# A routed mixture of experts on one core: the second layer with the rows on the partitions

## What is computed

```python
logits = (xf @ Wr + br) / TAU
top_val, top_idx = jax.lax.top_k(logits, 2)
top_w = jax.nn.softmax(top_val, axis=-1)
w = jnp.einsum('nke,nk->ne', jax.nn.one_hot(top_idx, E), top_w)
h = jnp.einsum('nd,edh->enh', xf, We1) + be1[:, None, :]      # 128 -> 768
a, g = jnp.split(h, 2, axis=-1)
act = a * gelu(g)
yE = jnp.einsum('enh,ehd->end', act, We2) + be2[:, None, :]   # 384 -> 128
yr = jnp.einsum('end,ne->nd', yE, w)
x = x + layernorm(ys + yr)
```

## Time and profile before

| | us |
|---|---|
| runs shown | 1186.52, 1187.3, 1191.24 |
| median | 1187.3 |
| the profiled execution: its own time | 1182.42 |
| its span, first to last instruction | 1180.7 |
| busy in the span: PE, DVE, ACT, POOL | 1019.0, 830.3, 742.6, 632.6 |

### The profile page before, as it was taken

How to read it: one execution, slowest core, us unless ns; L and a number is a source line. 1 busy time by engine, 2 the same in 40 slices (tenths; PEclk the granted TensorE clock), 3 DMA queues, 4 the chain that set the end, 5 groups by cost and what they waited for, 6 DMA issues and landing times. The chain is left out here.

```text
span 1180.7 us, 31510 instructions
## 1 busy us (share of the span) xinstructions
PE 1019.0 (86%) x8446; PEld 608.8 (52%) x8446; DVE 830.3 (70%) x2411; ACT 742.6 (63%) x1311; POOL 632.6 (54%) x1195
## 2 busy tenths in 40 slices
PE   4488888988888898987788998866999999999875
PEld 3453333333333333333345665535888888888732
DVE  5677887778777877777779998433666666666637
ACT  4577777777777767775655666414666666666616
POOL 4236666666666666664423777771444444444344
PEclk9899999999999999998996999878999999999988
DMA  8313333333332333333243111112222222221166
GB/s 217 94 47 93 99 96 103 95 100 87 97 108 86 99 95 99 100 99 111 71 150 115 54 54 57 54 60 68 61 64 64 64 58 63 62 65 54 43 224 210
DMA packets 135606, 107.47 MB, mean 91 GB/s; under 512 B 32203, under 2 KB 127874, under 8 KB 135538
## 3 DMA queue, kind: packets, MB, share of 16 engines
q1 hardware_dynamic: 124722, 87.45, 26.3%
q0 software_dynamic: 8544, 17.78, 4.2%
q10 hardware_dynamic: 2272, 1.45, 0.4%
HBM read 55.96 MB, written 50.69 MB: 90 GB/s over the span
## 5 line engine op out<-in xcount | busy, mean ns | idle before, releaser
L1542 DVE TENSOR_REDUCE maxima<-ps 128x8 f32<-128x1024 f32 x320 | 381.2, 1220 | 119.4 <-PE ps L1164 107.3
L916 ACT ACTIVATE pT_area<-ps 128x1024 f32<-128x1024 f32 x320 | 327.1, 1024 | 138.0 <-PE ps L1196 136.8
L704 POOL TENSOR_SCALAR_AFFINE_SELECT pT_area<-pT_area 128x256 f32<-128x256 f32 (+1 forms) x448 | 190.3, 439 | 103.7 <-ACT pT_area L916 103.2
L806 POOL DMA_INDIRECT ys_dram<-quad_area,place_cur x139 | 133.0, 957 | 192.6 <-issue 135.7
L1237 PE MATMUL ps<-pT_area,quad_area 128*32 128x512 f32 (+3 forms) x2048 | 190.7, 446 | 0.0
L796 POOL DMA_INDIRECT xs_dram<-quad_area,idx_cur x128 | 123.1, 962 | 74.9 <-issue 73.6
L1196 PE MATMUL ps<-quad_area 64*128 64x512 bf16 (+3 forms) x1024 | 125.5, 302 | 39.4 <-DVE maxima L1542 37.9
L1404 PE MATMUL ps<-quad_area 128*128 128x256 f32 (+1 forms) x456 | 130.0, 367 | 6.3 <-issue 4.5
L1405 PE MATMUL ps<-quad_area 128*128 128x256 f32 (+1 forms) x456 | 128.5, 364 | 0.0
L1164 PE MATMUL ps<-quad_area 61*128 61x128 bf16 (+2 forms) x1792 | 126.2, 242 | 0.0
L1024 ACT ACTIVATE xnT<-ps,be_cur 128x256 f32<-128x256 f32 (+1 forms) x228 | 94.4, 447 | 47.6 <-PE ps L1405 47.3
(11 more groups left out here) (237 smaller groups left out, 1523.1 us busy)
## 6 DMA issues: line engine op xcount, KB each, us to landing
qk_dram<-split_area SPq DMA_DIRECT2D x192, 128.0 KB, 2.3
quad_area<-qk_dram SPq DMA_DIRECT2D x256, 96.0 KB, 2.3
row_area<-xs_dram SPq DMA_DIRECT2D x63, 132.0 KB
pT_area<-ys_dram SPq DMA_DIRECT2D x16, 512.0 KB, 5.0
pT_area<-in_L_ffn_We SPq DMA_DIRECT2D x12, 384.0 KB, 7.0
out_dram<-pT_area SPq DMA_DIRECT2D x7, 512.0 KB, 2.9
xs_dram<-row_area SPq DMA_DIRECT2D x5, 528.0 KB, 4.2
split_area<-in_L_ffn_We SPq DMA_DIRECT2D x12, 192.0 KB, 3.6
```

Source lines behind the costliest of these rows:

```text
L704: return pool.affine_select(out=blocks, in_=blocks, compare_op=ALU.is_ge, fill=0.0, base=0, pattern=[[0, count], [1, P]], channel_multipli ...
L806: pool.indirect_dma_start(ys_dram, at, ys[:, ns % 2, h, :], None).then_inc(s_yst[ns % 2], 16)
L916: act.activation(pT[:, gs % 2, n, :], ps[:, bank:bank + 2, :].rearrange("p a b -> p (a b)"), ACT.Exp).then_inc(s_exp, 1)
L1542: dve.tensor_reduce(to, ps[:, bank:bank + 2, :].rearrange("p a (j k) -> p a j k", k=P), AX, ALU.max).then_inc(s_mxf, 1)
```

## The change

The experts' second layer swaps its operands: the hidden numbers are stationary, 128 rows at a time, and the weights `w2_cur` move, so a pair takes six matmuls of 128 columns instead of three of 256, and the result has the rows on the partitions at once. It goes into two PSUM banks in turn (`Y_BANKS`). The turn back (L1424), ACT's copy to `ysT` (L1034) and the wait chain through them go. The bias, which stood on the partitions, now stands along the columns: `be2` is loaded once, repeated on all partitions (`be2_all`, 128x1536, one DMA more on SP behind the weights), DVE copies the tile's 128 columns to `be2_cur` in each step, and the weighting becomes two operations, an add of the bias and a multiplication by the weight in place. `be_cur` loses a column. `routed_as` has four operations instead of five.

The order of a step changes on three engines. PE turns the rows of tile s+1 ahead of the first layer of tile s. ACT reads the next expert's number and copies the turned rows ahead of its gelus. DVE starts with the copies of the second-layer weights and bias of tile s, goes on with the three hidden products, weights tile s-2, and ends with `routed_as` of tile s+1, which waits for the scatter of tile s-3.

The diff, without the counts and names that follow from it (semaphores, buffers, waits on the number of small loads):

```diff
@@ -57,7 +57,7 @@
-YT_BANK, Y_BANK = 6, 7
+Y_BANKS = (6, 7)
@@ -217,7 +217,8 @@
-yT = v_flat[:, 1024:2048].rearrange("p (a t) -> p a t", a=2)
+yT = v_flat[:, 512:1536].rearrange("p (a t) -> p a t", a=2)
+be2_all = v_flat[:, 1536:1536 + E * C]
@@ -568,6 +569,8 @@
+    sp.dma_start(be2_all, a["L0_ffn_be2"].rearrange("(o e) c -> o (e c)", o=1).broadcast_to([P, E * C])).then_inc(s_we, 16)
+
@@ -799,7 +802,7 @@
-            pool.wait_ge(s_wt, 5 * n - 8)
+            pool.wait_ge(s_wt, 4 * n - 7)
@@ -1000,15 +1003,16 @@
-    act.activation(beT[:, :, 7], iota_f[:, ROUTED:ROUTED + E], ACT.Copy)
-    act.activation(beT[:, :, 6], ps[:, BE_TURN, 6 * E:7 * E], ACT.Copy).then_inc(s_beTsb, 1)
+    act.activation(beT[:, :, 6], iota_f[:, ROUTED:ROUTED + E], ACT.Copy).then_inc(s_beTsb, 1)
...
-    act.wait_ge(s_we, 16 * 2 * E)
-
-    def copy_w1(ns, n):
-        e = act.value_load(etile[0:1, bass.ds(n, 1)], min_val=0, max_val=E - 1)
+    act.wait_ge(s_we, 16 * (2 * E + 1))
+
+    def expert_of(n):
+        return act.value_load(etile[0:1, bass.ds(n, 1)], min_val=0, max_val=E - 1)
+
+    def copy_w1(ns, e):
@@ -1016,6 +1020,9 @@
     def expert_tile(ns, n):
+        if ns + 1 < ROUTED:
+            e = expert_of(n + 1)
+            copy_xsT(ns + 1, n + 1)
         if ns < ROUTED:
@@ -1024,17 +1031,9 @@
                 act.activation(gelE[:, ring, 0:width(ns)], ps[:, ring, 0:width(ns)], ACT.Gelu,
                                bias=be_cur[:, ns % 8, 3 + k:4 + k]).then_inc(s_ge, 1)
                 if k == 0 and ns + 1 < ROUTED:
-                    copy_w1(ns + 1, n + 1)
-        if ns + 1 < ROUTED:
-            copy_xsT(ns + 1, n + 1)
-        if 0 <= ns - 1 < ROUTED:
-
-            act.wait_ge(s_yeT, n)
-            w = width(ns - 1)
-            act.activation(ysT[:, (ns - 1) % 2, 0:w], ps[:, YT_BANK, 0:w], ACT.Identity,
-                           bias=be_cur[:, (ns - 1) % 8, 6:7]).then_inc(s_yeTsb, 1)
-
-    copy_w1(0, 0)
+                    copy_w1(ns + 1, e)
+
+    copy_w1(0, expert_of(0))
     copy_xsT(0, 0)
     expert_steps(act, expert_tile)
@@ -1393,6 +1392,8 @@
     def expert_tile(ns, n):
+        if ns + 1 < ROUTED:
+            turn_rows(ns + 1, n + 1)
         if ns < ROUTED:
@@ -1404,24 +1405,17 @@
                           start=True, stop=True).then_inc(s_he, 1)
-        if ns + 1 < ROUTED:
-            turn_rows(ns + 1, n + 1)
         if 0 <= ns - 1 < ROUTED:
-            par, w = (ns - 1) % 2, width(ns - 1)
+            par = (ns - 1) % 2
             pe.wait_ge(s_w2c, n)
-            ge(pe, s_yeTsb, n - 1)
+            ge(pe, s_yeb, n - 2)
             for k in range(CHUNKS):
                 pe.wait_ge(s_hide, CHUNKS * (n - 1) + k + 1)
-                last = pe.matmul(ps[:, YT_BANK, 0:w], w2_cur[:, par, k * P:(k + 1) * P], hidT[:, par, k, 0:w],
-                                 start=(k == 0), stop=(k == CHUNKS - 1))
-            last.then_inc(s_yeT, 1)
-        if 0 <= ns - 2 < ROUTED:
-
-            pe.wait_ge(s_yeTsb, n - 1)
-            ge(pe, s_yesb, n - 2)
-            for h in range(halves(ns - 2)):
-                last = pe.transpose(ps[:, Y_BANK, h * P:(h + 1) * P], ysT[:, ns % 2, h * P:(h + 1) * P], ident[:])
+                for h in range(halves(ns - 1)):
+                    last = pe.matmul(ps[:, Y_BANKS[par], h * C:(h + 1) * C], hidT[:, par, k, h * P:(h + 1) * P],
+                                     w2_cur[:, par, k * C:(k + 1) * C], start=(k == 0 and h == 0),
+                                     stop=(k == CHUNKS - 1 and h == halves(ns - 1) - 1))
             last.then_inc(s_ye, 1)
@@ -1812,47 +1806,58 @@
         ring, h = ns % 4, slice(0, halves(ns))
         to, other = weight_cur[:, ring, h], weight_other[:, ring, h]
-        second = xs[:, ring, h, SECOND_E]
+        second_e, expert = xs[:, ring, h, SECOND_E], be_cur[:, ns % 8, 6:7]
         dve.wait_ge(s_xs[ring], 32 * (n // 4 + 1) if isinstance(n, int) else 8 * (n - ring) + 32)
-        dve.tensor_scalar(second, second, be_cur[:, ns % 8, 7:8], None, ALU.is_equal).then_inc(s_wt, 1)
-        wait_apart(dve, s_wt, 5 * n + 1, s_passed)
         if ns >= 4:
             wait_apart(dve, s_yst[ns % 2], stored(ns - 4, n - 4), s_passed)
-        dve.tensor_tensor(place_cur[:, ring, h], xs[:, ring, h, PLACE], second, ALU.add).then_inc(s_wt, 1)
-        dve.tensor_tensor(to, xs[:, ring, h, SECOND_W], second, ALU.mult).then_inc(s_wt, 1)
-        dve.scalar_tensor_tensor(out=other, in0=second, scalar=0.0, in1=xs[:, ring, h, FIRST_W],
+        dve.scalar_tensor_tensor(out=place_cur[:, ring, h], in0=second_e, scalar=expert, in1=xs[:, ring, h, PLACE],
+                                 op0=ALU.is_equal, op1=ALU.add).then_inc(s_wt, 1)
+        dve.scalar_tensor_tensor(out=to, in0=second_e, scalar=expert, in1=xs[:, ring, h, SECOND_W],
                                  op0=ALU.is_equal, op1=ALU.mult).then_inc(s_wt, 1)
-        wait_apart(dve, s_wt, 5 * n + 4, s_passed)
+        dve.scalar_tensor_tensor(out=other, in0=second_e, scalar=expert, in1=xs[:, ring, h, FIRST_W],
+                                 op0=ALU.not_equal, op1=ALU.mult).then_inc(s_wt, 1)
+        wait_apart(dve, s_wt, 4 * n + 3, s_passed)
         dve.tensor_tensor(to, to, other, ALU.add).then_inc(s_wt, 1)
+
+    def copy_second(ns, n):
+
+        ge(dve, s_ye, n - 1)
+        e = dve.value_load(etile[0:1, bass.ds(n, 1)], min_val=0, max_val=E - 1)
+        dve.tensor_copy(w2_cur[:, ns % 2, :], we2[:, bass.ds(e * HR, HR)]).then_inc(s_w2c, 1)
+        dve.tensor_copy(be2_cur[:, ns % 4, :], be2_all[:, bass.ds(e * C, C)]).then_inc(s_b2c, 1)
     def expert_tile(ns, n):
         if ns < ROUTED:
             par, w = ns % 2, width(ns)
-            routed_as(ns, n)
+            copy_second(ns, n)
             for k in range(CHUNKS):
                 ring = (CHUNKS * ns + k) % H_BANKS
                 dve.wait_ge(s_ge, CHUNKS * n + k + 1)
-                if k == 0:
-                    ge(dve, s_yeT, n - 1)
                 dve.scalar_tensor_tensor(out=hidT[:, par, k, 0:w], in0=ps[:, ring, RT:RT + w], scalar=be_cur[:, ns % 8, k:k + 1],
                                          in1=gelE[:, ring, 0:w], op0=ALU.add, op1=ALU.mult).then_inc(s_hide, 1)
-            ge(dve, s_yeT, n - 1)
-            e = dve.value_load(etile[0:1, bass.ds(n, 1)], min_val=0, max_val=E - 1)
-            dve.tensor_copy(w2_cur[:, par, :], we2[:, bass.ds(e * HR, HR)]).then_inc(s_w2c, 1)
         if 0 <= ns - 2:
-
-            par, h = ns % 2, halves(ns - 2)
-            dve.wait_ge(s_ye, n - 1)
-            wait_apart(dve, s_wt, 5 * n - 5, s_passed)
-            if ns >= 4:
-                dve.wait_ge(s_yst[par], stored(ns - 4, n - 4))
-            dve.tensor_tensor(ys[:, par, 0:h], ps[:, Y_BANK, 0:P * h].rearrange("p (h c) -> p h c", h=h),
-                              weight_cur[:, (ns - 2) % 4, 0:h].rearrange("p (h o) -> p h o", o=1).broadcast_to([P, h, C]),
-                              ALU.mult).then_inc(s_yesb, 1)
-
-    dve.wait_ge(s_we, 16 * 2 * E)
+            weigh(ns - 2, n - 2)
+        if ns + 1 < ROUTED:
+            routed_as(ns + 1, n + 1)
+
+    def weigh(ns, n):
+
+        par, h = ns % 2, halves(ns)
+        to, w = ys[:, par, 0:h], weight_cur[:, ns % 4, 0:h]
+        bias = be2_cur[:, ns % 4].rearrange("p (o c) -> p o c", o=1).broadcast_to([P, h, C])
+        dve.wait_ge(s_ye, n + 1)
+        wait_apart(dve, s_b2c, n + 1, s_passed)
+        wait_apart(dve, s_wt, 4 * n + 4, s_passed)
+        if ns >= 2:
+            dve.wait_ge(s_yst[par], stored(ns - 2, n - 2))
+        dve.tensor_tensor(to, ps[:, Y_BANKS[par], 0:C * h].rearrange("p (h c) -> p h c", h=h), bias, ALU.add).then_inc(s_yeb, 1)
+        wait_apart(dve, s_yeb, n + 1, s_passed)
+        dve.tensor_tensor(to, to, w.rearrange("p (h o) -> p h o", o=1).broadcast_to([P, h, C]), ALU.mult).then_inc(s_yesb, 1)
+
+    dve.wait_ge(s_we, 16 * (2 * E + 1))
     for par in range(2):
         dve.wait_ge(s_scat[par], 8 * R * B)
+    routed_as(0, 0)
     expert_steps(dve, expert_tile)
```

More of the change, by code:

```diff
@@ L256, in build @@
         outT = outT_area[:, 0:2 * T].rearrange("p (a t) -> p a t", a=2)
-        be_rows = sb("be_rows", [E * 7, P])
-        beT = sb("beT", [P, E, 8])
-        be_cur = sb("be_cur", [P, 8, 8])
+        be_rows = sb("be_rows", [E * 6, P])
+        beT = sb("beT", [P, E, 7])
+        be_cur = sb("be_cur", [P, 8, 7])
         rows_cur = quad_area[:, 0:DEPTH * NT * ROW].rearrange("p (a t c) -> p a t c", a=DEPTH, c=ROW)
@@ L265, in build @@
         hidT = quad_area[:, 0:2 * CHUNKS * RT].rearrange("p (a k t) -> p a k t", a=2, k=CHUNKS)
-        xsT, ysT = (quad_area[:, at:at + 2 * RT].rearrange("p (a t) -> p a t", a=2) for at in (2048, 3072))
+        xsT = quad_area[:, 2048:2048 + 2 * RT].rearrange("p (a t) -> p a t", a=2)
         ys = quad_area[:, 4096:4096 + 2 * RT].rearrange("p (a h c) -> p a h c", a=2, h=2)
@@ L269, in build @@
         w2_cur = outT_area[:, 0:2 * HR].rearrange("p (a x) -> p a x", a=2)
```

(20 more changed lines are left out.)

## The result

The changed kernel takes 1204.74 us, median of four runs (1201.76 to 1206.77), against 1186.91 for the kernel before on the same chip: a ratio of 1.0158, 95% interval 1.0135 to 1.018. It is slower by 1.6%; the forecast was 0.9%, and of the 17.8 us between the two medians it had summed up 10.4. The profiled execution took 1205.39 us, of which 1203.6 is span.

A forecast was written before the change was run, and what follows sets the result against it. PE was taken to bound the pairs before, DVE's loops through the scatter after. Pairs +2, handover +1.5, singles +3.9, drain +1.5 and late scatters +1.5 made +10.4: 1192.8 profiled, 1197.7 us median, range 1182 to 1209.

The forecast's parts named there:

- With both loops turning: Pairs: the one-step loop holds the row load where the two-step loop needs it, so steps take about 4.36 us.
- Loop two: Two steps: weighting, scatter, place (4.84 to 5.42 us), then DVE's stretch to the next weighting (3.71): 4.28 to 4.57 a step.
- the pairs: 60 steps of the experts' stage, two tiles' weightings apart: 4.36 us against 4.33, so +2 us (-3 to +10).
- loop one: One step: place, routing, SP's row load, delayed scatter, next place; 4.24 to 4.30 us before, 4.30 to 4.36 after.
- PE's 4.15 can't be had while this loop stands: Pairs: the one-step loop through row load and scatter, 4.30 to 4.36 us, keeps PE from its 4.15 step.
- Rival A: PE sets the pace: scatter clear of the row load, pairs at 4.15 us, singles break even; 1176.5 us, chance 0.12.
- about where they meet: Pairs: 4.36 us a step, where the one-step and two-step loops through the scatter were taken to meet.
- late scatters: Around the loop's exit a few scatters land late, no longer hidden by PE's pace: +1.5 us (0 to 4).
- The singles: Nine steps after the pairs: DVE takes over from ACT's chain, 3.3 us a step against 2.87, so +3.9 us.
- Handover and drain: Last pair to first single, 11.7 us against 10.2; last singles to last landing, 10.4 against 8.9: +1.5 each.
- PE's saving: Pairs: PE's step falls from 4.33 to 4.15 us, 0.18 less, 10.8 over 60 steps if PE sets the pace.
- Rival C: DVE's two copies hold up POOL's scatter issue by 0.56 us, pairs +13 in place of +2; 1209 us, chance 0.15.

The follow-up runs named there:

- e3: Changed kernel, with SP's row load also waiting for the scatter of tile s-4, so it starts after that landing: 1193.32 us, ratio 1.0071 to the kernel before.
- e1: Changed kernel with eight slots for the places instead of four, so a place waits for the scatter of eight tiles earlier: 1180.44 us, ratio 0.9959 to the kernel before.
- e2: Changed kernel with DVE's register load issued behind the hidden products, a step ahead of the copies using it; four slots: 1181.42 us, ratio 0.9964 to the kernel before.
- e5: Changed kernel with DVE's register load and both copies put back behind the hidden products; four slots: 1177.25 us, ratio 0.9935 to the kernel before.
- e4: Changed kernel with both eight slots for the places and the register load behind the hidden products: 1170.03 us, ratio 0.9872 to the kernel before.
- e8: Changed kernel with DVE's register load done twice in a row ahead of the copies: 1221.89 us, ratio 1.0306 to the kernel before.
- e7: Changed kernel with eight slots and early register load, but rows turned behind the first layer and copied behind ACT's gelus: 1170.12 us, ratio 0.9876 to the kernel before.

## Why the prediction was right, and where it was off

The direction was forecast, and so was the wait that binds; the size was not: +10.4 us were summed, and the stage took 18.9 more.

**What binds.** "With both loops turning" was half right. Loop two binds as described, and its stretch measures as summed: place to weighting 3.66 and 3.76 against 3.71. The parts err both ways: place to the end of the register load is 1.51 (908.34 to 909.85) against 0.55 + 0.7, the copies 0.41 (909.85 to 910.26) against 0.56, the hidden products 1.18 against 1.28, add to multiplication 0.56 against 0.62. e3 shows that the scatter and its collision with the row load are the other half of that loop, e1 that without the wait nothing of the pairs' loss is left.

**The step that failed is loop one:** "PE's 4.15 can't be had while this loop stands". It stands unchanged in e2 and e5, and PE has its 4.15 to 4.2 there. Its two rows showed the row load holding up a place by 2.6 to 2.7; that the load, coming later step by step, falls behind the scatter and lets a place through was not thought of. Rival A named an escape by an earlier row load; e3 makes that one by hand, and e2 and e5 show one by a later. The trace of before has the later one too, behind a weighting at 861.77 (SP and DVE):

```profile
864.94 0.38 SPq L582 DMA_DIRECT2D row_area<-xs_dram  x1
...
866.97 0.16 DVE L1821 TENSOR_TENSOR place_cur<-row_area 128x2 int32<-128x2 f32 x1 [0.26 <-DVE row_area L1817]
```

The row load starts 3.17 behind the weighting, and the place comes 2.03 behind the row load without waiting for the scatter, where the prediction held that no row shows less than 2.6. It is rare there: PE's 4.33 is longer than loop one's 4.24 to 4.30, so the row load mostly drifts the other way, from 2.80 behind the weighting (tile 21) to 2.35 (tile 28).

**The term that was mis-sized is the pairs.** 4.36, "about where they meet", came from that loop. Loop two by itself was summed at 4.28 to 4.57, and the steady steps from tile 14 to tile 54 measure 4.435, with 5.17 from a weighting to its place and 3.70 from there to the next weighting: the scatter is caught by the row load in part in most steps, about half of the way from 4.84 to 5.42. That is +6.6 us over 60 steps where +2 was put down, inside the bounds of 4.28 to 4.50. On top of it come the late scatters of the first and last steps, +4.4 where +1.5 was put down, just over the 4 allowed: the 14 steps from tile 0 take 65.5 us where 14 of 4.435 are 62.1, and the six from tile 54 to 60 take 27.6 for 26.6.

**The singles** were forecast at 3.3 and take 3.43 a step, by the chain through DVE's queue that was forecast. In the changed kernel's DVE timeline:

```profile
1117.56 0.29 DVE L1855 TENSOR_TENSOR quad_area<-quad_area,weight_cur 128x128 f32<-128x128 f32 x1
...
1119.15 0.60 DVE L1826 COPY outT_area<-split_area 128x384 f32 x1 [0.60 <-PE ps L1416]
...
1120.99 0.29 DVE L1855 TENSOR_TENSOR quad_area<-quad_area,weight_cur 128x128 f32<-128x128 f32 x1
```

The prediction's terms add up to 3.3 to 3.5, of which it took the lower end. The copy of 0.36 takes 0.60 there, which it didn't have, and the gap of the register load is 0.60 in place of 0.7; here too the view names PE. The first single's step, with a place that still waits for a scatter of the pairs, takes 4.14, and nine steps take 31.8. **Handover and drain** came out as summed: 11.7 against 11.7, and from the weighting at 1138.29 to the last landing 10.5 against 10.4, the last scatter in the chain being:

```profile
1146.55 2.22 DMA ys_dram<-quad_area,place_cur
```

**PE's saving** of 0.18 a step is real: 4.15 in e4 against the 4.15 worked out. It is 10.7 of the 15 us by which e4's stage is shorter than that of the kernel before; singles and handover make up most of the rest.

**Rival C** gave 1209, nearer to the result than the forecast, but not by its mechanism. Copies do meet POOL's issues (909.85 and 910.12 meet 909.91) and the issue takes 1.13 there in place of 0.957, so POOL pays a little, 0.17 at most in the changed kernel, not the 0.56 of both copies. Of the issue by line, ns min/median/max, in the changed kernel and in e4; in the kernel before it is 952/957/970:

```profile
L809 POOL DMA_INDIRECT ys_dram<-quad_area,place_cur x139: 952/957/1127, 825.5 to 1146.6; - x139
```

```profile
L809 POOL DMA_INDIRECT ys_dram<-quad_area,place_cur x139: 954/1021/1174, 824.1 to 1111.4; - x139
```

The Trainium skill (SBUF — State Buffer, "SBUF: two separate sides") has it that of such a copy and POOL the one that starts first keeps the other out for its whole length. The rows agree in the order, since only the one that starts second gets longer: the issue at 909.91, and in the singles the copy at 1119.15, where the issue (from 1118.63) keeps its 0.96. They differ in the size: the issue at 909.91 is 0.17 longer where 0.30 of the copy was left, and that copy 0.24 longer where 0.44 of the issue was left. In e4 the copy meets the first issue of each pair, mostly by starting ahead of it; half of the issues are longer, and no kernel here is faster.

## What to carry to other kernels

A wait that is often seen but hidden is still one side of a loop. Before an edit shortens the engine that hides it, add up the whole loop, over as many steps as it has (weighting to landing, and on to the next weighting), and divide by those steps: here that sum, 4.28 to 4.57, held the measured 4.435, and the bound read from two rows of one part of it did not hold. The register load from SBUF cost 0.60 to 0.72 us where nothing long was queued ahead of it on its engine; behind three products it left no gap in 61 of e5's 76 steps. Its place alone decided between 1.6% slower (the changed kernel) and 0.4% faster (e2), and with the copies behind it 0.7% faster (e5).

## What the runs showed of the hardware that was not expected

**Of a copy and an indirect issue that meet, the second one stretches.** Where the DVE copy of 128x384 starts 0.05 us or more ahead, POOL's issue goes from 0.957 up to 1.14 and the copy keeps its 0.36. Where the issue starts first, or at the same time to 0.04, the copy goes up to 0.61 and the issue, in all meetings but three, keeps its 0.957. In the ten traces no meeting has made both of them longer.

**A row load holds up a scatter only at some distances.** In the steady steps of the kernel before, the changed one, e2 and e5 a place that waits stands 4.8 to 5.0 behind its weighting where the row load started 2.0 to 2.1 behind it, 5.4 to 5.6 at 2.8, 5.5 to 5.7 at 2.9, and 4.9 to 5.1 again from 3.05 to 3.15.

**A scatter's landing can be 1.9 us late beside an instruction transfer.** In the changed kernel the place at 857.93 waits 2.10, until 6.81 after the weighting (851.12) whose scatter it needs, where 5.1 to 5.5 is usual. The scatter's second half, issued at 853.60, took 4.20 to land, where the median is 2.25:

```profile
857.93 0.22 DVE L1813 SCALAR_TENSOR_TENSOR place_cur<-row_area,be_cur 128x2 int32<-128x2 f32 x1 [2.10 <-DMA ys_dram<-quad_area,place_cur]
```

The DMA view from 855.3 to 856 us has one packet of instructions there (packets, MB, share of 16 engines):

```profile
q8 instruction: 1, 0.02, 11.8%
```

A packet on that queue stands at 874.81 as well, inside the other late landing (issued at 873.15, 3.70), and none from 890 to 1040, where no place was late. In the traces that show landings (before, changed, e1 in part, e3, e8) all seven landings of more than 3.5 us have such a packet inside. Other packets stand inside landings that were on time, and no run here took the transfers away, so the cause stays open. In the kernel before such landings were mostly hidden behind PE.

The late place of tile 60 (1082.52, 6.90 behind its weighting) has another reason. POOL issued the second half of tile 56 late, 3.17 us behind the first half, where 1.26 is usual:

```profile
1076.82 0.96 POOL L809 DMA_INDIRECT ys_dram<-quad_area,place_cur  x1 [2.02 <-issue]
1080.00 1.11 POOL L809 DMA_INDIRECT ys_dram<-quad_area,place_cur  x1 [2.22 <-issue]
```

All ten traces have this at the same tile (3.49 in e7, 3.17 in the others), in the third step behind the loop; what POOL does there no run shows.

**One step in eight is 0.4 us longer** where PE doesn't bind, at the branch between two bodies of the loop of eight (L392 in DVE's queue): 4.80 to 4.88 in the steady part of the changed kernel, 4.83 in e3. The step after it takes 4.11 in the changed kernel and gives most of it back. The gap ahead of the copy, 0.70 in the other steps, holds the branch there as well:

```profile
923.54 0.36 DVE L1826 COPY outT_area<-split_area 128x384 f32 x1 [1.16 <-PE ps L1416]
```
